# Row stores three quads later in the transfer queue, the next batches' inputs loaded a block earlier, and a run of GpSimd subtractions moved forward

## Chip, core and metric

The kernel runs on one core of a Trainium2 chip. The metric is the device time of one execution in microseconds (us), taken as the median of several runs. A profiled execution is one run of its own, with its own time.

The core's engines are TensorE (PE in the rows, PEld for its weight loads), VectorE (DVE), ScalarE (ACT), GpSimd (POOL) and SyncE (SP), which here only issues transfers and waits. Each engine has one instruction queue and works through it in order; engines meet at semaphores.

## What is computed

Four batches of 512 tokens of width 128 go through four pairs of a cross attention (to 32 context tokens) and a feed-forward part. The last feed-forward part is a mixture of 64 experts, six per token:

```
    x = x + jnp.tanh(g_xattn[0]) * _L0_xattn_ref(_layernorm(x, axis=-1), ctx_1024, mask_BxS2_bk0, ...)
    x = x + jnp.tanh(g_ffn[0]) * _L0_ffn_ref(_layernorm(x, axis=-1), ...)
    x = x + jnp.tanh(g_xattn[1]) * _L1_xattn_ref(_layernorm(x, axis=-1), ctx_1024, mask_BxSxS2_if1, ...)
    ...
    x = x + jnp.tanh(g_ffn[3]) * _L3_ffn_ref(_layernorm(x, axis=-1), ...)

            h = jax.nn.silu(jnp.einsum('th,eih->eti', x, eg_w)) * jnp.einsum('th,eih->eti', x, eu_w)
            routed = jnp.einsum('eti,ehi,te->th', h, ed_w, comb)
```

## The kernel before

The program is a sequence of blocks. In a block (`block_of`) a main part and side parts are woven together on each engine by hand-written step numbers: a part says `yield n`, and a side's piece due at step n is put into the queue when the main part reaches that step. At a block's end all engines meet. SP's program of a block is written out by itself: `first_loads`, then the clearing of one set of semaphores, then `sync`.

**Blocks 1 and 2, the front.** `fronts_beside_setup` runs `front` (the first cross attention, the first feed-forward part with its rounding to four bits, `fp4_quantise`, and the second cross attention) for batches 0 and 1, with `setup`, which prepares weights. `fronts_beside_route` runs `front` for batches 2 and 3, with `route_1`. The two fronts of a block are interleaved; in the rows of block 1, `work`, `region_a`, `weights` and `pt` belong to batch 1 (called A below), and `turned`, `small_f` and `rows` to batch 0 (B). `load_inputs` loads five arrays for a batch: context, turned context, two masks, and x. `front` begins by waiting for all five. `setup` on POOL scales small weights and then subtracts a row of the first expert matrix `w1` from its other rows, one 128x512 subtraction for each of eight experts (L649).

**The expert pages of the last layer.** Tokens have been scattered to HBM in the order of their experts (`sorted_3`). `pages_3` works on 28 quads of four pages of 128 rows. For quad q, PE turns the rows (`turn_rows`, L2899), multiplies each page with its expert's two matrices (`up`, L2911), two quads later turns the hidden rows (`turn_hidden`, L2922), and three quads later (DOWN_LAG) multiplies them down (`down`, L2935). ACT copies the turned rows (L2957), applies silu (L2963) and copies the turned hidden rows (L2970). DVE multiplies (L2987, L2995) and copies the result of a quad to SBUF (`copy_sum`, L3002). SP loads the rows of a quad (L2855) and stores its results to `made_3` (L2889). Rows and results have three buffers each. PE's order for a step q is page 0 to 3 of up(q), turn_hidden(q-2), down(q-3), with turn_rows(q+1) put between page 2 and page 3. SP's queue is

```
                for q in range(QUADS_3):
                    if q >= 3:
                        sp.wait_ge(s.xt, q - 2)
                        load_pages_3(sp, s, q)
                    n = q - DOWN_LAG - 1
                    if n >= 0:
                        store_rows(sp, n)
```

where `s.xt` counts turned quads, and `store_rows` waits for `copy_sum(n)`. Beside the pages runs `back` for the last batch (the third feed-forward part's experts and the fourth cross attention), with its steps three pages apart (`paced`).

Of the kernel before, what the change touches and what calls it, by code (L numbers as in the profile page):

```python
# [17 lines left out]
I32 = mybir.dt.int32  # L18
# [7 lines left out]
K = 32  # L26
NK2 = S + K
E8 = 8
# [19 lines left out]
QUADS_3 = (K6 * GT3 + E3) // 4  # L48
# [20 lines left out]
def flamingo_kernel(nc, a, at, early_at, out):  # L69
    with ExitStack() as ctx:  # L70
# [27 lines left out]
        def bank(i, n=1):  # L98
            return psum[:, 512 * i:512 * (i + n)]
# [12 lines left out]
        def part(region, offset, shape):  # L112

            n = int(np.prod(shape[1:]))
            v = region[0:shape[0], offset:offset + n]
            if len(shape) == 3:
                v = v.rearrange("p (a b) -> p a b", a=shape[1])
            if len(shape) == 4:
                v = v.rearrange("p (a b c) -> p a b c", a=shape[1], b=shape[2])
            return v  # L120
# [122 lines left out]
        def front_tail_of(acc):  # L243
# [9 lines left out]
                       mask1=part(turned, 1536, [P, T, K]).bitcast(I32))  # L253
# [21 lines left out]
        def back_norm(region, offset):  # L275
# [21 lines left out]
        lg = sb("lg", [P, T, E3])  # L297
        lge = sb("lge", [P, T, E3])
        gmask = sb("gmask", [P, T, 8])
        comb = sb("comb", [P, T, E3])  # L300
# [11 lines left out]
                       big_f=part(wide_2, 0, [P, T, 512]), kblk1=part(wide_2, 2048, [P, H1, K]), vo1=part(wide_2, 2560, [P, 4, D]),  # L312
                       qt_f=xnt, pt_f=part(ysb_flat, 0, [P, 2, 512]), y1_f=y1s[0], vblk1=part(wide_2, 3072, [P, H1, K]),
                       mask1=part(ysb_flat, 0, [P, T, K]).bitcast(I32))
        w_at = front_tail + FRONT_SMALL
        front_w2 = record(stats=part(region_a, w_at, [P, T, 6]), mv=part(region_a, w_at + 24, [P, T, 2]),
                          rstd=part(region_a, w_at + 32, [P, T]), rtmp=part(region_a, w_at + 36, [P, T]),
# [162 lines left out]
        def load_first_matrices(sp, s):  # L480

            for e in range(E8):
                sp.dma_start(w1[:, e, 0:F1], a["w1"][:, e, :]).then_inc(s.w1_in, 16)
                sp.dma_start(last_row(e), a["w1"][D - 1:D, e, :].broadcast_to([D, F1])).then_inc(s.w1_in, 16)

        def clear_sorted(sp, s):

            sp.wait_ge(s.cleared, 1)
            for rows in sorted_1:
                sp.dma_start(rows.rearrange("(n p r) d -> p n (r d)", p=P, r=4),  # L490
                             over(kctx[:, :, :].rearrange("p c k -> p (c k)"), 1, [P, PAGES // 4, 4 * D])).then_inc(s.rows_out, 16)

        def setup(s):
# [135 lines left out]
            def gpsimd(pool):  # L629
                yield 0  # L630
                nc.gpsimd.memset(neg_half[:, :], -0.5)
                nc.gpsimd.memset(mean_col[:, :], 1.0 / F1).then_inc(s.zeroed, 1)
                pool.wait_ge(s.front_in, all_front)
                nc.gpsimd.tensor_scalar(bq1s[:, :], bq1[:, :], float(HD1) ** -0.5, None, ALU.mult)
                nc.gpsimd.tensor_scalar(wq0s[:, :], bq0[:, :], float(D) ** -0.5, None, ALU.mult).then_inc(s.small, 1)
                yield 11
                pool.wait_ge(s.moe1_in, 16)
                nc.gpsimd.tensor_scalar(g1s[:, :], g1[:, :], float(F1) ** 0.5, None, ALU.mult).then_inc(s.g1_scaled, 1)
                pool.wait_ge(s.rest_in, all_rest)
                nc.gpsimd.tensor_scalar(rtmp[:, 0:1], wl1[:, :], 0.125, None, ALU.mult).then_inc(s.wl1_scaled, 1)  # L640
                nc.gpsimd.tensor_scalar(wgate2[:, :], wgate2[:, :], wl2[:, 0:1], None, ALU.mult)
                nc.gpsimd.tensor_scalar(wg2[:, :, :], wg2[:, :, :], wl2[:, 0:1], None, ALU.mult)
                nc.gpsimd.tensor_scalar(wu2[:, :, :], wu2[:, :, :], wl2[:, 0:1], None, ALU.mult)
                nc.gpsimd.tensor_scalar(sgu2[:, :, :], sgu2[:, :, :], wl2[:, 0:1], None, ALU.mult)
                for e in range(E8):
                    yield 20 + e
                    if e == 0:
                        pool.wait_ge(s.w1_in, 16 * 2 * E8)
                    nc.gpsimd.tensor_tensor(w1[:, e, 0:F1], w1[:, e, 0:F1], last_row(e), ALU.subtract)  # L649

            return record(tensor=tensor, vector=vector, scalar=scalar, gpsimd=gpsimd)
# [2206 lines left out]
        def pages_3(s, s_late):  # L2858

            gate_up = region_a[:, 0:2 * CH3 * 512].rearrange("p (a n) -> p a n", a=2)  # L2860
            TURN_LAG, DOWN_LAG = 2, 3
# [13 lines left out]
            def sync(sp):  # L2875
                for q in range(QUADS_3):
                    if q >= 3:
                        sp.wait_ge(s.xt, q - 2)
                        load_pages_3(sp, s, q)
                    n = q - DOWN_LAG - 1  # L2880
                    if n >= 0:
                        store_rows(sp, n)
                for n in range(QUADS_3 - DOWN_LAG - 1, QUADS_3):
                    store_rows(sp, n)

            def store_rows(sp, n):
# [190 lines left out]
        def fronts_beside_setup():  # L3077
            k = next_block()
            s0 = sems(k % 2, SETUP)
            sf = sems(k % 2, FRONT, s0)  # L3080
            sg = sems(k % 2, FRONT, sf)

            def sync(sp):
                load_front_weights(sp, s0)
                load_inputs(sp, sf, 0, front_1)
                load_inputs(sp, sg, 1, front_2)
                load_other_weights(sp, s0)
                load_first_matrices(sp, s0)
                clear_sorted(sp, s0)
                sp.wait_ge(s0.rows_out, 32)  # L3090
            block_of(k, sync, front(sf, 0, bank(0), front_1, set_f), [setup(s0), front(sg, 1, bank(3), front_2, front_w2)])

        def fronts_beside_route():
            k = next_block()
            sf = sems(k % 2, FRONT)
            sg = sems(k % 2, FRONT, sf)
            sr = sems(k % 2, ROUTE_1, sg)
            sw = sems(k % 2, ("table_in",), sr)
            s_pages = sems(1 - k % 2, PAGES_1)

            def first_loads(sp):
                load_inputs(sp, sf, 2, front_1)
                load_inputs(sp, sg, 3, front_2)

            def sync(sp):
                sp.wait_ge(sf.inputs, 5 * 16)
                sp.wait_ge(sg.inputs, 5 * 16)
                lo = early_at["b1"][0]
                sp.dma_start(w1[D - 1:D, :, 0:F1],
                             a["early"][0:E8, lo:lo + F1].rearrange("(o e) f -> o e f", o=1)).then_inc(sw.table_in, 16)  # L3110
                lo = at["be2"][0]
                sp.dma_start(be2_rows[:, :, :], over(a["weights"][0:E8, lo:lo + D], 0, [P, E8, D])).then_inc(sw.table_in, 16)
                sp.wait_ge(sw.table_in, 32)
                sp.wait_ge(scattered_1[0], 16 * K1 * GT)
                for q in range(3):
                    load_pages(sp, s_pages, q)
            block_of(k, sync, front(sf, 2, bank(0), front_1, set_f),
                     [front(sg, 3, bank(1), front_2, front_w2), route_1(sr, 0, bank(2), lambda n: 2 * n, 4)], first_loads)

        def moe_1_pages():  # L3120
            k = next_block()
# [103 lines left out]
        for b in range(B):  # L3225
            k = next_block()
# [121 lines left out]
```

## Time and profile before

| | |
|---|---|
| median of 3 runs | 1887.72 us (1884.27 to 1894.0) |
| profiled execution, its own time | 1881.52 us |
| its span, first to last instruction | 1879.7 us |
| mean granted TensorE clock | 0.929 |
| PE busy | 1614.8 us (86%) |
| DVE, POOL, ACT busy | 62%, 45%, 41% |
| block 1 | about 0.7 to 111.2 us |
| block of the expert pages | about 1569 to 1785.6 us |

A busy share says how long an engine had an instruction in work, not what the end waited for. The granted clock is 1.0 at 2.4 GHz and 0.5 at 1.2 GHz.

### The profile page before, as it was taken

The page shows a single profiled execution, that of the slowest core. Times are in us where ns is not written, and L with a number is a line of the kernel's source. Part 1 is how long each engine was busy: PE and PEld are TensorE (multiplying, and loading weights), DVE is VectorE, ACT ScalarE, POOL GpSimd, SP SyncE. Part 2 cuts the span into 40 slices and gives each one's busy share as a digit, 9 for nine tenths or more (in the row PEclk, how much of TensorE's full clock was granted, in tenths as well). Part 3 has the DMA queues.
Part 4 walks back from the last instruction along what each step waited for, and adds up shares of the span by engine and source line. Part 5 has one row for each costly group of instructions (what it writes and reads, how often), then busy time and mean ns, then how long its engine had stood idle before and what let it go on. Part 6 is the DMA issues. An engine that isn't in the chain of part 4 may idle for free. (4 is left out here: it accounts for less than half of the span.)

```text
span 1879.7 us, 30972 instructions
## 1 busy us (share of the span) xinstructions
PE 1614.8 (86%) x10175; PEld 1106.4 (59%) x10175; DVE 1171.0 (62%) x3120; ACT 772.6 (41%) x1974; POOL 848.6 (45%) x1075
## 2 busy tenths in 40 slices
PE   6755699899999999998999978699899996776699
PEld 4544477557756577564775645456577565555556
DVE  6957569767566577564784754677477473332357
ACT  2321244356446465373661742222366274222222
POOL 3441744357565386571874730127266471000072
PEclk8866799999999999999999979799999998877899
DMA  9010122100000500000000010144000004222253
GB/s 332 17 28 1 39 88 77 35 6 7 1 1 2 164 8 1 1 1 2 11 1 1 2 46 1 51 150 134 12 1 1 18 2 157 68 59 65 80 156 116
DMA packets 79564, 91.34 MB, mean 49 GB/s; under 512 B 10872, under 2 KB 57592, under 8 KB 78480
## 3 DMA queue, kind: packets, MB, share of 16 engines
q1 hardware_dynamic: 74288, 78.86, 13.6%
q0 software_dynamic: 5120, 10.50, 1.9%
q8 instruction: 86, 1.41, 0.3%
q14 instruction: 70, 0.57, 0.1%
HBM read 69.14 MB, written 27.66 MB: 51 GB/s over the span
## 5 line engine op out<-in xcount | busy, mean ns | idle before, releaser
L1672 POOL TENSOR_TENSOR rows<-rows,rinv 128x512 f32<-128x512 f32 x192 | 198.7, 1063 | 117.2 <-DVE rinv L1912 117.2
L1836 ACT ACTIVATE rows<-psum,nmax 128x512 f32<-128x512 f32 x192 | 130.0, 683 | 122.1 <-DVE nmax L1905 122.0
L2021 POOL TENSOR_TENSOR rows<-rows,rinv 128x128 f32<-128x128 f32 (+2 forms) x192 | 127.4, 685 | 77.9 <-DVE rinv L2190 77.9
L1904 DVE TENSOR_REDUCE lg<-psum 128x2 f32<-128x1024 f32 x128 | 155.7, 1216 | 3.2
L2185 DVE TENSOR_REDUCE nmax<-psum 128x1 f32<-128x128 f32 (+3 forms) x256 | 113.6, 485 | 42.7 <-PE psum L2067 41.7
L1916 DVE COPY turned<-psum 128x512 f32<-128x512 f32 x128 | 88.2, 689 | 80.3 <-PE psum L1732 79.3
L1720 PE MATMUL psum<-region_a,region_b 64*128 64x256 f32 x1024 | 130.6, 391 | 6.0 <-ACT rows L1836 2.9
L1753 PE MATMUL psum<-turned,region_a 128*64 128x256 f32 x1024 | 124.6, 385 | 0.4
L2064 PE MATMUL psum<-region_a,region_b 64*128 64x128 f32 (+2 forms) x896 | 107.2, 353 | 9.8 <-ACT rows L2137 3.7
L1720 PEld LDWEIGHTS psum<-region_a,region_b 64*128 64x128 f32 x1024 | 92.8, 186 | 28.9 <-ACT rows L1836 7.7
L1732 PEld LDWEIGHTS psum<-weights,rows 128*128 128x128 f32 x768 | 82.0, 140 | 44.9 <-issue 20.7
L1732 PE MATMUL psum<-weights,rows 128*128 128x128 f32 x768 | 103.3, 279 | 3.8 <-ACT turned L1845 2.4
L2137 ACT ACTIVATE rows<-psum,nmax 128x128 f32<-128x128 f32 (+2 forms) x192 | 96.1, 509 | 12.1 <-DVE nmax L2185 12.1
L1753 PEld LDWEIGHTS psum<-turned,region_a 128*64 128x64 f32 x1024 | 68.6, 136 | 47.1 <-issue 19.6
L2579 ACT ACTIVATE region_b<-psum 128x512 f32<-128x512 f32 x66 | 39.4, 598 | 138.0 <-PE psum L2541 138.0
L1845 ACT ACTIVATE turned<-psum 128x512 f32<-128x512 f32 x128 | 76.7, 599 | 46.0 <-PE psum L1732 46.0
L2064 PEld LDWEIGHTS psum<-region_a,region_b 64*128 64x128 f32 x896 | 70.2, 189 | 34.1 <-issue 11.8
L2553 PEld LDWEIGHTS psum<-region_c,region_b 128*128 128x128 f32 x512 | 66.0, 192 | 28.0 <-issue 22.7
L2079 PE MATMUL psum<-weights,rows 128*128 128x128 f32 x448 | 76.6, 281 | 6.8 <-DVE region_a L2196 1.7
L2987 DVE TENSOR_TENSOR region_b<-region_b,psum 128x256 f32<-128x256 f32 x28 | 11.8, 421 | 110.3 <-ACT region_b L2963 110.2
L1698 PE MATMUL psum<-kvt,weights 128*128 128x512 f32 x128 | 65.8, 643 | 11.3 <-PEq L760 7.7
L2957 ACT ACTIVATE weights<-psum 128x512 f32<-128x512 f32 x28 | 16.7, 597 | 135.4 <-PE psum L2899 135.4
(853 smaller groups left out, 4040.5 us busy)
## 6 DMA issues: line engine op xcount, KB each, us to landing
pt<-gates SPq DMA_DIRECT2D x64, 128.0 KB
ysb<-gates SPq DMA_DIRECT2D x64, 128.0 KB
weights<-sorted SPq DMA_DIRECT2D x28, 256.0 KB, 3.2
made<-weights SPq DMA_DIRECT2D x28, 256.0 KB, 2.4
sorted<-sorted SPq DMA_DIRECT2D x4, 1536.0 KB, 13.5
region_a<-in_eg SPq DMA_DIRECT2D x16, 256.0 KB, 4.3
region_a<-in_eu SPq DMA_DIRECT2D x16, 256.0 KB, 3.6
region_c<-in_weights SPq DMA_DIRECT2D x16, 256.0 KB, 5.7
```

The lines of the kernel that those rows point to most:

```text
L1672: nc.gpsimd.tensor_tensor(row(u, j), row(u, j), rinv[:, 2 * u + j:2 * u + j + 1].broadcast_to([P, S]), ALU.mult).then_inc(s.pn, 1)
L1720: mm = nc.tensor.matmul(s_bank(u, j)[:, 256 * half:256 * (half + 1)], qtt[lo:lo + 64, p, P * t:P * (t + 1)], ktt[lo:lo + 64, p, 256 * half ...
L1732: mm = nc.tensor.transpose(turn_bank(place(n, i))[:, P * k:P * (k + 1)], row(u, j)[:, P * k:P * (k + 1)], ident[:, :])
L1753: nc.tensor.matmul(bank(7)[lo:lo + HD2, 256 * half:256 * (half + 1)], vtok[:, k, P * p + lo:P * p + lo + HD2], turned2[:, 2 * half + j, k, :],
L1836: nc.scalar.activation(row(u, j), s_bank(u, j), ACT.Exp, bias=nmax[:, 2 * u + j:2 * u + j + 1], accum_out=sum_column(u // T, u % T, j)).th ...
L1845: nc.scalar.activation(turned_to(n, i), turn_bank(place(n, i)).rearrange("p (k q) -> p k q", q=P), ACT.Copy).then_inc(s.ca, 1)
L1904: link(nc.vector.tensor_reduce(maxima(u // T)[:, both(u), 0], both_scores(u), AX.X, ALU.max, negate=True))
L1916: nc.vector.tensor_copy(turned_to(n, i), turn_bank(place(n, i)).rearrange("p (k q) -> p k q", q=P)).then_inc(s.cb, 1)
L2021: nc.gpsimd.tensor_tensor(head, head, rinv[:, 2 * u + j:2 * u + j + 1].broadcast_to([P, keys(u)]), ALU.mult).then_inc(s.pn, 1)
L2064: nc.tensor.matmul(s_bank(u, j)[:, cols], qtt[lo:lo + 64, p, P * t:P * (t + 1)], krot[lo:lo + 64, cols], start=(h == 0), stop=True, skip_g ...
L2137: nc.scalar.activation(rows_of(u)[:, j, 0:keys(u)], s_bank(u, j)[:, 0:keys(u)], ACT.Exp, bias=nmax[:, 2 * u + j:2 * u + j + 1], accum_out= ...
L2185: nc.vector.tensor_reduce(nmax[:, 2 * u + j:2 * u + j + 1], s_bank(u, j)[:, 0:keys(u)], AX.X, ALU.max, negate=True).then_inc(s.mx, 1)
```

## The change

There are three edits.

First, in `pages_3` SP puts the store of quad n behind the load of quad n + 7, where it stood behind the load of quad n + 4. The waits are the same ones.

Second, block 1 loads the inputs of batches 2 and 3 behind its own loads. They go to arrays that block 1 does not use (`lg`, `lge`, `comb`); the x of batch 3 lies on weights that `setup` reads, so SP first waits for the two products that read them (`kv_products`). The clearing of `sorted_1` stands behind that wait now. `first_loads` of block 2 is gone, and its fronts read the new places.

Third, the eight subtractions on `w1` stood at steps 20 to 27 of block 1 and stand at step 12.

```
+        def next_inputs(n):
+            return dict(ctx_tok=lg[0:K, 2 * n:2 * n + 2, :].rearrange("p t e -> p (t e)"), ctx_t=lge[:, n, 0:K],
+                        mask0=lge[:, n, K:2 * K].bitcast(I32),
+                        mask1=comb[:, 2 * n:2 * n + 2, :].rearrange("p t (h k) -> p (t h) k", h=2).bitcast(I32))
+
+        front_3, front_4 = dict(front_1, **next_inputs(0)), dict(front_2, **next_inputs(1))
...
+                yield 12
+                pool.wait_ge(s.w1_in, 16 * 2 * E8)
                 for e in range(E8):
-                    yield 20 + e
-                    if e == 0:
-                        pool.wait_ge(s.w1_in, 16 * 2 * E8)
                     nc.gpsimd.tensor_tensor(w1[:, e, 0:F1], w1[:, e, 0:F1], last_row(e), ALU.subtract)
...
-                    n = q - DOWN_LAG - 1
+                    n = q - DOWN_LAG - 4
                     if n >= 0:
                         store_rows(sp, n)
-                for n in range(QUADS_3 - DOWN_LAG - 1, QUADS_3):
+                for n in range(QUADS_3 - DOWN_LAG - 4, QUADS_3):
                     store_rows(sp, n)
...
+                sf_next = sems(1 - k % 2, FRONT)
+                load_inputs(sp, sf_next, 2, front_3)
+                sp.wait_ge(s0.kv_products, 2)
+                load_inputs(sp, sems(1 - k % 2, FRONT, sf_next), 3, front_4)
                 clear_sorted(sp, s0)
                 sp.wait_ge(s0.rows_out, 32)
...
-            def first_loads(sp):
-                load_inputs(sp, sf, 2, front_1)
-                load_inputs(sp, sg, 3, front_2)
...
-            block_of(k, sync, front(sf, 2, bank(0), front_1, set_f),
-                     [front(sg, 3, bank(1), front_2, front_w2), route_1(sr, 0, bank(2), lambda n: 2 * n, 4)], first_loads)
+            block_of(k, sync, front(sf, 2, bank(0), front_3, set_f),
+                     [front(sg, 3, bank(1), front_4, front_w2), route_1(sr, 0, bank(2), lambda n: 2 * n, 4)])
```

The new code stands five or more lines lower in the file, so the same instruction has a higher line number after. On SP, at the start of the page block, the queue before is this (`weights<-sorted_3` is a load of a quad's rows, `made_3<-weights` a store; even_5 counts turned quads, even_14 copied results):

```order
L2473 DMA region_c<-in_weights 128x512 x8
L84 ISA x65
L2855 DMA weights<-sorted_3 128x4x128 [waits even_5] x2
L2889 DMA made_3<-weights 128x4x128 [waits even_14]
L2855 DMA weights<-sorted_3 128x4x128 [waits even_5]
```

and with the change it is this:

```order
L2478 DMA region_c<-in_weights 128x512 x8
L84 ISA x65
L2860 DMA weights<-sorted_3 128x4x128 [waits even_5] x5
L2894 DMA made_3<-weights 128x4x128 [waits even_14]
L2860 DMA weights<-sorted_3 128x4x128 [waits even_5]
```

Five loads stand ahead of the first store where two stood; from there on loads and stores alternate in both, and at the end eight stores follow one another where five did.

On POOL, in block 1, the queue from the scaled weights to the softmax of the second attention (L1088 subtracts a maximum, L1093 multiplies with a reciprocal) is before:

```order
L643 TENSOR_SCALAR weights<-weights 128x512
L644 TENSOR_SCALAR weights<-weights 128x128
L669 TENSOR_SCALAR region_a<-region_a 128x4
L670 TENSOR_TENSOR region_a<-region_a,neg_half 128x4
L669 TENSOR_SCALAR rtmp_f<-mv_f 128x4
L670 TENSOR_TENSOR rstd_f<-rtmp_f,neg_half 128x4
L649 TENSOR_TENSOR region_a<-region_a,region_c 128x512 x4
L1088 TENSOR_TENSOR weights<-weights,region_a 128x512
L1088 TENSOR_TENSOR rows<-rows,small_f 128x512
L649 TENSOR_TENSOR region_a<-region_a,region_c 128x512
```

and with the change:

```order
L649 TENSOR_SCALAR weights<-weights 128x512
L650 TENSOR_SCALAR weights<-weights 128x128
L654 TENSOR_TENSOR region_a<-region_a,region_c 128x512 x6
L654 TENSOR_TENSOR region_a<-region_a,region_b 128x512 x2
L674 TENSOR_SCALAR region_a<-region_a 128x4
L675 TENSOR_TENSOR region_a<-region_a,neg_half 128x4
L674 TENSOR_SCALAR rtmp_f<-mv_f 128x4
L675 TENSOR_TENSOR rstd_f<-rtmp_f,neg_half 128x4
L1093 TENSOR_TENSOR weights<-weights,region_a 128x512
L1093 TENSOR_TENSOR rows<-rows,small_f 128x512
```

All eight subtractions stand ahead of the two reciprocal deviations (L669 and L670 before); four of them stood behind those, and four stood singly in the softmax.

On SP, at the end of block 1, the queue before ends with the clearing, and block 2 begins with ten loads:

```order
L484 DMA region_b<-in_w 128x512
L490 DMA sorted_0<-kctx 128x6x512
L490 DMA sorted_1<-kctx 128x6x512
L760 UNCONDITIONAL_BRANCH
L761 UNCONDITIONAL_BRANCH
L456 DMA turned<-in_ctx 32x128
L456 DMA small_f<-in_ctx_t 128x32
L456 DMA small_f<-in_mask_keys 128x32
L456 DMA turned<-in_mask_BxSxS_if 128x4x32
L456 DMA x<-in_x 128x4x128
```

With the change, the last rows of block 1 and the first of block 2 are:

```order
L462 DMA lge<-in_ctx_t 128x32
L462 DMA lge<-in_mask_keys 128x32
L462 DMA comb<-in_mask_BxSxS_if 128x4x32
L462 DMA weights<-in_x 128x4x128
L496 DMA sorted_0<-kctx 128x6x512
L496 DMA sorted_1<-kctx 128x6x512
L765 UNCONDITIONAL_BRANCH
L766 UNCONDITIONAL_BRANCH
L84 ISA x65
L3114 DMA region_a<-in_early 1x8x512
```

The ten loads stand ahead of the clearing now, and block 2 begins with the clearing of its semaphores.

## Rows read from the trace of the kernel before

**Rows 1.** PE's waits, 1597 to 1773.1: line, releaser, us, times, longest.

```profile
PE psum L2899 <- DMA weights<-sorted: 47.4, 22, 3.8
PE psum L2935 <- ACT region_b L2970: 8.3, 12, 3.6
PE psum L2911 <- ACT weights L2957: 2.5, 9, 0.3
```

**Rows 2.** Windows: length, busy PE, PEld, DVE, ACT, POOL (instructions), clock, DMA share, GB/s.

```profile
1579.72:1587.41 7.69, 6.36 (x52) 5.54 (x50) 4.89 (x17) 3.12 (x7) 0.00 (x0) 1.00 0.17 47
1597.80:1773.02 175.22, 118.86 (x627) 97.54 (x627) 55.70 (x114) 38.57 (x77) 2.47 (x4) 0.80 0.24 67
```

**Rows 3.** Timeline, SP, DVE and PE, one quad: start, duration, engine, instruction, idle before.

```profile
1754.74 0.36 SPq L2889 DMA_DIRECT2D made<-weights  x1
1755.14 0.51 SPq L2855 DMA_DIRECT2D weights<-sorted  x1
...
1758.38 0.66 PE L2899 MATMUL psum<-weights 128*128 128x128 f32 x4 [2.23 <-DMA weights<-sorted]
...
1766.03 0.44 PE L2899 MATMUL psum<-weights 128*128 128x128 f32 x2 [3.76 <-DMA weights<-sorted]
```

**Rows 4.** Transfers by line: count, KB each, median us from issue to landing.

```profile
weights<-sorted SPq DMA_DIRECT2D x28, 256.0 KB, 3.2
made<-weights SPq DMA_DIRECT2D x28, 256.0 KB, 2.4
```

**Rows 5.** PE groups, 1597.80 to 1773.02: busy us, mean ns, idle before.

```profile
L2922 PE MATMUL psum<-weights,region_b 128*128 128x128 f32 x88 | 29.3, 333 | 0.0
```

**Rows 6.** Timeline, PE, pages at the lower and the full clock.

```profile
1616.64 0.63 PE L2911 MATMUL psum<-region_a,weights 128*128 x2
...
1617.71 0.64 PE L2911 MATMUL psum<-region_a,weights 128*128 x2
...
1760.99 0.39 PE L2911 MATMUL psum<-region_a,weights 128*128 x2
...
1761.55 0.39 PE L2911 MATMUL psum<-region_a,weights 128*128 x2
```

**Rows 7.** Timeline, seam of blocks 1 and 2: DVE, SP, PE.

```profile
110.71 0.48 DVE L1053 SCALAR_TENSOR_TENSOR x<-turned,gate,x 128x256 f32<-128x256 f32 x1
119.25 0.28 DVE L956 BATCH_NORM_STATS2 region_a<-pt 32x6 f32<-32x128 f32 x1 [8.05 <-DMA weights<-in_x]
...
111.47 0.34 SPq L456 DMA_DIRECT2D turned<-in_ctx  x1
```

**Rows 8.** Timeline, POOL, block 1.

```profile
49.97 0.76 POOL L644 TENSOR_SCALAR weights<-weights 128x128 f32<-128x128 f32 x1
65.42 0.23 POOL L669 TENSOR_SCALAR region_a<-region_a 128x4 f32<-128x4 f32 x1 [14.69 <-DVE region_a L662]
...
69.29 4.94 POOL L649 TENSOR_TENSOR region_a<-region_a,region_c 128x512 f32<-128x512 f32 x4
...
92.57 1.27 POOL L649 TENSOR_TENSOR region_a<-region_a,region_b 128x512 f32<-128x512 f32 x1
```

**Rows 9.** Timeline, DVE, block 1: the same operations alone and beside POOL.

```profile
51.02 0.17 DVE L415 TENSOR_SCALAR small_f<-small_f 128x16 f32<-128x16 f32 x1
...
54.51 0.43 DVE L425 TENSOR_SCALAR turned<-turned 128x512 f32<-128x512 f32 x1
...
67.80 1.08 DVE L680 TENSOR_SCALAR work<-x,region_a 128x128 f32<-128x128 f32 x4
69.36 4.95 DVE L680 TENSOR_SCALAR turned<-x,mv_f,rstd_f 128x128 f32<-128x128 f32 x4 [0.48 <-POOL rstd_f L670]
```

**Rows 10.** Timeline, PE, block 1.

```profile
71.20 0.60 PE L877 MATMUL psum<-weights,work 128*128 128x128 f32 x4
74.46 1.09 PE L877 MATMUL psum<-weights,turned 128*128 128x128 f32 x4 [2.66 <-DVE turned L680]
```

**Rows 11.** SP's waits, 0 to 160: line, releaser, us, times, longest.

```profile
SPq L760 <- PEq L760: 60.5, 1, 60.5
```

## The prediction

> **What bounds the kernel now.** PE is the busiest engine, so I first read what PE waits for, stage by stage, and then who releases it. In the block of the expert pages PE waits 22 times, 47.4 us in all, in front of L2899 (the turning of the next quad's rows) for the transfer that brings those rows; its two other waits there, for ACT, come to 10.8 us [rows 1]. No other stage has a wait for data that returns so often. Second comes the clock: over the same 175 us the granted clock is 0.80, where in the quads before the first store it is 1.00 [rows 2]. Third, between block 1 and block 2, DVE stands 8.05 us until the last input of batch 3 has landed [rows 7]. All three lie on the chain that sets the end: the block of the pages ends with PE, and every block starts when the last engine has left the one before.
>
> **Why the loads are late.** The SP queue says it. A store and the next load go out one behind the other, 1754.74 and 1755.14, and PE gets its rows at 1758.38, 3.24 us after the load's issue [rows 3]; the median landing time of a load is 3.2 us [rows 4]. That load was free to go long before: its buffer is empty once the quad three before has been turned. What held it was the store in front of it, which waits for a result made at the very step in which the next quad is turned. So each quad pays the landing time less the work of two or three pages.
>
> **The stores moved back.** Load of quad m now stands behind the store of quad m-8, whose result is copied at the start of step m-4, and waits for the turning of quad m-3, in the middle of step m-4. It goes out in the middle of step m-4 and is needed in the middle of step m-1, three quads later. A plain quad takes 7.65 - 3.76 = 3.89 us without its wait (1758.38 to 1766.03, [rows 3]), so the load has more than 11 us for 3.2 us of landing. The wait goes wholly: -47.4 us. The stores themselves are issued when they were, at the result's copy; a result buffer is needed again three quads, again 11 us or more, after its store goes out, and a store lands in 2.4 us [rows 4]. The last eight stores wait for their own results as the last five did, so the end of the block gets no tail. No instruction is added.
>
> **What the clock gives.** L2922 takes 0.27 us at the full clock and 0.42 us at the lower (2.4 and 1.2 GHz). Its mean over 88 is 333 ns [rows 5], so (333 - 270) / 150 = 42% of the pages ran at the lower one. Two successive pages start 1.07 us apart there (1616.64, 1617.71) and 0.56 us apart at full clock (1760.99, 1761.55) [rows 6]. 88 x 0.42 x 0.51 = 19 us for the pages; turning and `back` add about 10 by my count of their slower rows. The falls of the clock stand behind waits of 2 us and more. With PE busy 83% of the time (6.36 of 7.69 us) the clock was 1.00 [rows 2]. Without the waits PE would be busy 86% or more, so I expect most of this 29 us to come back. But not as time: a page at full clock meets waits for ACT of about 0.5 us a quad that the slower page hides. I build the stage from both sides. Upper end of the stage: no clock regained, 175.2 less the 45.6 us of waits inside it (47.4 less the first, 1.81) = 129.6 us. Lower end: 22 quads x 3.89 = 86 us, plus `back` on PE at full clock, 19 us by the starts of its rows, plus 3 us for the longest wait behind ACT (3.6 in [rows 1]) that stays = 108 us. Faster quads also pull the steps of `back` together, three pages being 1.7 us at least; each of its links (PE, then ACT or DVE for 0.6 to 0.7 us, then PE) fits, its softmax does not quite. I add 5 us for that, and 3 us for a clock that still falls at such places: 116 us. The term is 116 - 175.2 - 1.8 = **-61 us**, bounds -47 and -69.
>
> By the Trainium skill ("TensorE: Matmul & The Clock Gate", section "What's actually happening") the lower clock is the default and activity releases it, which speaks for the -61. A reader who distrusts it has -47 from the waits alone.
>
> **The inputs loaded ahead.** SP gave its first load at 111.47 and DVE started at 119.25 [rows 7]. With all arrays in place DVE and PE can start about half a microsecond behind SP's first row, at 112.0: -7.2 us. Block 2 is a chain from there to its scatter, so it shifts as a whole. The cover: the first load set goes behind the `w1` loads; the second and the clearing wait for a product that PE ends near 54 us; SP stood 60.5 us at the block's end waiting for PE [rows 11], so starting the clearing 20 us later costs nothing. Bounds -8 and 0 (if the last set came late after all).
>
> **The subtractions moved.** POOL is idle 14.69 us behind L644, from 50.7 on [rows 8], and the eight subtractions of 1.24 us each (4.94 for four) fill 50.7 to 60.7. POOL is not late for its next piece at 65.4. The price is on DVE. Four 128x128 operations of one source take 1.08 us alone and 4.95 us beside four subtractions: one per subtraction [rows 9]. In 51.0 to 54.9 DVE has exactly eight such operations (L415 to L425) on the chain to PE's L865. Held one by one they end with the eighth subtraction, at 60.7 and not 54.94: +5.7 us. Behind them PE is late: L865, L870, then L535's 64 products, and L877 of A, which started right behind them at 71.20, comes at 76.9. The hold of the four operations at 69.36 is gone, so L877 of B follows at once, at 77.8 where it stood at 74.46 [rows 10]: +3.4 us. In the softmax POOL is nearly full, and the subtraction at 92.57 [rows 8] stands in front of the product that PE waits for at 98: -1.3. Sum +2.1; bounds -4 (no hold, both savings kept) and +6.
>
> The Trainium skill ("GPSIMD Engine Reference", section 1, Specifications) says that POOL shares its SBUF interfaces with DVE instructions in a two-port mode or with two SBUF inputs. By it L421 is held as well: ninth in the row, some 0.4 us more, +2.5 for +2.1. It speaks against this edit, as the rows do.
>
> **Sum.** -61 - 7.2 + 2.1 = -66 us. Made against the profiled execution: 1881.5 - 66 = 1815.5. The median of the runs is 6.2 us above it: **1822 us**.
>
> **The rivals.**
> 1. The clock does not come back (chance 0.20). For: it has waits behind ACT to fall at, 10.8 us of them. Against: 1.00 in the quads without stores. Gain 47 + 5 - some 5 us of new waits in `back`: 1841 us.
> 2. `back` becomes the bound of the pages (0.09). Its links are serial over PE, ACT and DVE, and PE's wait for rows has hidden them. If the block only falls by 35 us: 1888 - 35 - 5 = 1848 us. Against: DVE is busy 55.7 and ACT 38.6 of 175 us.
> 3. DVE's hold reaches further (0.10): also the twelve small scalings behind L1017 and the next norm are late, or the inputs of batch 3 come late. The front then is +6 for -5: 1833 us.
> 4. More than forecast (0.08): the clock stays full and `back` fits everywhere; -69 - 8: 1810 us.
> 5. The other side, slower (0.02): result buffers. A store that went out later than its result would hold `copy_sum` three quads on, and with it PE's L2935. It decides only if the store is delayed past 9 us (three quads of 3.89 less 2.4); each quad then pays up to a whole landing, between 2.4 and 3.2 us [rows 4]. At 3.2 that is 24 x 3.2 = 77 us for the 47 gained, and with the front 1888 + 77 - 47 - 5 = 1913 us. Against: SP's wait ahead of each store is over before the store's own.
> 6. Nothing happens in the page block (0.02): the load's wait on turned quads is the true holder. 1883 us, as the front alone. Against: the order of SP's rows at each of 22 quads.
> The forecast has the remaining 0.49.
>
> **How the numbers follow.** The forecast's own range is 1814 to 1832. Rivals 1, 3 and 4 are neighbours, so 1808 to 1844 holds 8 in 10. A measurement of this kernel can tell about 0.5%, 9 us, from no change. Faster by more than that hold all but rivals 5 and 6: 0.96; within 0.5%: 0.02; slower: 0.02.
>
> **What would show it.** PE's wait for `weights<-sorted` falls from 47.4 us to under 3. The clock of the page block rises from 0.80 to 0.93 or more. The distance from the fifth quad's turning to the last is near 116 us; 130 means rival 1, 140 rival 2. In the SP rows a load is issued some 11 us before its L2899. DVE's first row of block 2 follows the last of block 1 within 1 us. DVE's eight small operations after 51 us stretch to 60 or 61; were they as short as before, the front would gain 10 us. The prediction is wrong if the page block's new waits on ACT or DVE pass 15 us.

## The result

| | before | changed |
|---|---|---|
| median of 4 runs | 1887.58 us (1884.27 to 1894.0) | 1814.12 us (1801.71 to 1816.75) |
| profiled execution, span | 1879.7 us | 1814.8 us |
| mean granted TensorE clock | 0.929 | 0.938 |

The ratio is 0.9594, with a 95% interval of 0.9542 to 0.9646: 73.5 us faster by the medians. The forecast was 1822 us in a range of 1808 to 1844. The total is near, but the page block gave more than was forecast and other parts less; what follows takes them apart.

The head of the changed kernel's profile page (busy time and share of each engine):

```profile
PE 1594.1 (88%) x10175; PEld 1088.8 (60%) x10175; DVE 1175.5 (65%) x3120; ACT 772.7 (43%) x1974; POOL 850.9 (47%) x1075
```

The number of PE instructions is the same as before (10175), and PE is 21 us less busy: no work went away, PE did the same matmuls at a higher clock. Most of the gain is in the page block. The waits of PE in it, first turning to last (line, releaser, us, times, longest); then the window from the sixth quad's turning to the last, with its clock in the third column from the right; then the groups that answer to [rows 4, 5]:

```profile
PE psum L2940 <- ACT region_b L2975: 13.5, 23, 3.6
PE psum L2916 <- ACT weights L2962: 4.8, 15, 0.6
PE psum L2916 <- DMA region_a<-in_eu: 4.4, 1, 4.4
PE psum L2904 <- PEq L2002: 2.3, 1, 2.3
```

```profile
1602.74:1708.04 105.30, 91.05 (x628) 75.69 (x628) 54.63 (x113) 38.33 (x77) 2.47 (x4) 0.96 0.36 106
```

```profile
L2927 PE MATMUL psum<-weights,region_b 128*128 128x128 f32 x92 | 25.8, 280 | 0.0
```

The waits for `weights<-sorted`, 47.4 us at L2899 in [rows 1], are gone: L2904 waits once, for the block to begin. The window of 22 quads is 105.3 us where [rows 2] has 175.22: PE stands idle 14.25 us in it instead of 56.36, and is busy 91.05 instead of 118.86. So of the 70 us gained 42 us are idle time of PE and 28 us are its higher clock. The matmul of L2927 takes 280 ns on average, 333 in [rows 5].

Three plain quads in the timeline of the changed kernel, SP and PE (start, duration, engine, instruction):

```profile
1657.33 0.60 PE L2904 MATMUL psum<-weights 128*128 128x128 f32 x4
1657.96 0.36 SPq L2860 DMA_DIRECT2D weights<-sorted  x1
1660.72 0.36 SPq L2894 DMA_DIRECT2D made<-weights  x1
1661.00 0.60 PE L2904 MATMUL psum<-weights 128*128 128x128 f32 x4
1661.63 0.36 SPq L2860 DMA_DIRECT2D weights<-sorted  x1
...
1664.67 0.60 PE L2904 MATMUL psum<-weights 128*128 128x128 f32 x4
...
1668.35 0.60 PE L2904 MATMUL psum<-weights 128*128 128x128 f32 x4
```

A load now follows the turning that empties its buffer (1657.33, 1657.96), and its store follows alone, 2.8 us later. The load of 1657.96 is turned at 1668.35, 10.4 us on, where [rows 3] has 3.24. A plain quad takes 3.67 us.

The front gained less. DVE, POOL and PE of the changed kernel in block 1, and DVE at the seam:

```profile
51.99 0.69 DVE L420 TENSOR_REDUCE small_f<-turned 128x16 f32<-128x512 f32 x1
52.71 0.97 DVE L421 TENSOR_SCALAR small_f<-small_f 128x16 f32<-128x16 f32 x1
...
56.17 0.25 DVE L425 RECIPROCAL small_f<-small_f 128x16 f32<-128x16 f32 x1
56.46 1.42 DVE L427 TENSOR_TENSOR turned<-turned,small_f 128x512 f32<-128x512 f32 x1
57.91 1.37 DVE L428 TENSOR_SCALAR turned<-turned 128x512 f32<-128x512 f32 x1
...
63.52 0.43 DVE L431 TENSOR_SCALAR turned<-turned 128x512 f32<-128x512 f32 x1
...
115.22 0.48 DVE L1058 SCALAR_TENSOR_TENSOR x<-turned,gate,x 128x256 f32<-128x256 f32 x1
116.01 0.28 DVE L961 BATCH_NORM_STATS2 region_a<-lg 32x6 f32<-32x128 f32 x1 [0.31 <-PEq L765]
```

```profile
52.39 8.01 POOL L654 TENSOR_TENSOR region_a<-region_a,region_c 128x512 f32<-128x512 f32 x6
60.36 2.84 POOL L654 TENSOR_TENSOR region_a<-region_a,region_b 128x512 f32<-128x512 f32 x2
```

```profile
79.92 0.60 PE L882 MATMUL psum<-weights,work 128*128 128x128 f32 x4
80.36 0.60 PE L882 MATMUL psum<-weights,turned 128*128 128x128 f32 x4
```

Between DVE's last row of block 1 and its first of block 2 lie 0.8 us where [rows 7] has 8.5. But block 1 ends at 115.2 and not at 110.7. The run of operations behind the reduction took 3.95 us before; it takes 11.3 us here, 52.68 to 63.95. Of its ten operations eight are held, each about as long as the subtraction beside it; the reciprocal (0.25 us) and the last one (0.43 us, behind the last subtraction) are not. The eight subtractions take 10.8 us, 1.35 us each for the 1.24 of [rows 8].

The same events in both profiled executions, before and changed: DVE's first row of block 2 119.25 and 116.01 (-3.2); the first load of `sorted_1`'s rows in block 3 224.21 and 222.01 (-2.2); SP's first copy of `sorted_1` to `sorted_3` 611.01 and 612.38 (+1.4); SP's first load of `in_eg` 1104.27 and 1104.49 (+0.2); the second load of `in_weights` to `region_c` 1208.99 and 1217.31 (+8.3); the page block's first turning 1569.02 and 1577.26 (+8.2); its last turning 1773.02 and 1708.04 (-65.0); POOL's first gather behind it 1788.06 and 1722.09 (-66.0); the span -64.9. So the page block with its end gave 74.2 us, and the 8 us at 1104 to 1209 are a loss in a place that the change does not touch. One window in it (length, busy PE ..., clock), of the changed kernel and of the one before:

```profile
1120.00:1150.00 30.00, 26.62 (x79) 13.20 (x78) 10.28 (x33) 10.84 (x19) 0.00 (x0) 0.71 0.00 1
```

```profile
1120.00:1150.00 30.00, 26.88 (x113) 13.89 (x112) 14.13 (x39) 12.22 (x20) 0.00 (x0) 0.97 0.00 1
```

PE is busy for the same 26.6 to 26.9 us, with 79 instructions in one and 113 in the other: the granted clock was 0.71 here and 0.97 there. Over the whole stretch (1104.49 to 1217.31 here, 1104.27 to 1208.99 there) both have 334 matmuls, and PE is busy 85.4 us here and 78.2 us there, at a clock of 0.77 and 0.83: 7.3 of the 8.1 us. It is not a property of the change: the same changed kernel on another chip (`c1_after` below) took 104.4 us for this stretch, at a clock of 0.83.

### The profile page after: what moved, and what is told of

Read it like the earlier page. It is cut to its first block and busy times, and to the rows that moved or that the text cites. A ratio compares the mean times of both kernels' runs of the same rounds, so it can differ in the third digit from the quotient of the medians.

```text
span 1814.8 us, 30972 instructions
## 1 busy us (share of the span) xinstructions
PE 1594.1 (88%) x10175; PEld 1088.8 (60%) x10175; DVE 1175.5 (65%) x3120; ACT 772.7 (43%) x1974; POOL 850.9 (47%) x1075
## 5 line engine op out<-in xcount | busy, mean ns | idle before, releaser
L2850 POOL DMA_INDIRECT sorted<-turned,small_f x48 | 49.2, 1024 | 49.6 <-DVE small_f L2784 35.2
L1689 POOL TENSOR_TENSOR ysb<-ysb,nmax 128x128 f32<-128x128 f32 x64 | 25.9, 405 | 94.8 <-DVE nmax L1910 93.9
## 6 DMA issues: line engine op xcount, KB each, us to landing
sorted<-sorted SPq DMA_DIRECT2D x4, 1536.0 KB, 13.7
```

## The experiments

Twelve runs were made in three groups (a "call" in the expectations), each group on a chip of its own, with the kernel before beside them. The kernel before had medians of 1992.6, 1893.0 and 1988.2 us there. So totals are compared inside a group, and stages between groups. The changed kernel itself ran only in the third group. "The stage" is the one from the sixth quad's turning to the last, 175.22 us before and 105.30 us changed.

### The stores alone

```diff
-                    n = q - DOWN_LAG - 1
+                    n = q - DOWN_LAG - 4
```

> The kernel before with the stores three quads later and nothing else. Theory A (the stores carry the whole gain): the stage from the sixth quad's turning to the last falls from 175.2 to 105 us as with the full change, PE's wait for weights<-sorted is gone, and the time is 1888 less 74 = 1814 us; DVE's first row of block 2 stays at 119. Theory B (the page block gave the 61 us that the prediction put on it and the rest came from elsewhere): 1827 us. Theory C (the clock of that stage was luck of the one profiled run): the stage at 0.80 again and 130 us long, 1841 us.

1915.15 us for 1992.64, 77.5 us less; ratio 0.9618, interval 0.9589 to 0.9648. The stage (same columns as above):

```profile
1649.45:1754.40 104.95, 90.65 (x627) 75.62 (x627) 54.63 (x113) 38.33 (x77) 2.46 (x4) 0.96 0.36 105
```

This is theory A. The stores alone carry the gain in the page block, on another chip, with the stage's clock at 0.96 again; what the other two edits add to the total is not told apart from nothing by the intervals (0.9618 here, 0.9592 for the full change in the third group). B (a ratio of 0.968) lies outside the interval, and C is out: the regained clock was no luck of one run.

### The inputs alone, and the subtractions alone

> The kernel before with the inputs of batches 2 and 3 loaded in block 1 and nothing else. Theory A: the ten loads cost block 1 nothing, its last DVE row stays at 110.7 and the first of block 2 comes at 111.5 to 112.0, 7.2 us earlier than before. Theory B: the loads are what made block 1 late by 1.7 us at 42 us (they are issued from 32.8 us on, beside the loads of the first matrices): the first row of block 2 comes at 113.2 to 113.7. In the page block nothing changes (stage 175 us).

> The kernel before with the eight subtractions at step 12 and nothing else. Theory A (the subtractions hold DVE one operation each, and their own length with it, 1.36 us, is what counts): DVE's held operations after 51 us end at 62.2 us where they ended at 54.94 before (+7.3), block 1 ends 2.8 us later, at 113.5, and DVE's first row of block 2 comes at about 122. Theory B (the 1.7 us by which block 1 was late at 42 us belong to the subtractions too): the held operations end at 63.9 and the block at 115.2. Theory C (the prediction's sum, +2.1): 112.8.

The inputs alone: 1983.99 us (one run). DVE's last row of block 1 starts at 112.71 and the first of block 2 at 113.50, 0.8 us apart; the kernel with the stores alone, on the same chip and with the old inputs, has 110.21 and 118.67, 8.5 us. The gap shrinks by 7.7 us. The block itself ended late, at theory B's number. The first 1.4 us of it are not shown to be the loads': the reduction at the head of B's quantising starts at 50.30 in the profile of before, 50.92 with the stores alone, 51.69 here and 51.75 with the subtractions alone, and that kernel loads nothing ahead. Behind B's L883 the block takes 36.9 us here and 35.1 us with the stores alone, with PE busy 28.1 and 26.5 us for the same 120 matmuls, so most of this 1.7 us is clock; why it was lower here is open. The stage of the pages is 176.94 us.

The subtractions alone: 1999.18 us (one run). The reduction starts at 51.75, and the last operation of the run ends at 63.72: 11.3 us behind the reduction's end, +7.3 again, the size in theory A. The times themselves are theory B's (63.9 and 115.2 were said; block 1's last row starts at 115.53), but the late start is not the subtractions', as the inputs alone have it too. Block 1 ends 5.3 us behind the kernel with the stores alone, and the first row of block 2 comes at 124.28 for 118.67. The stage of the pages is 180.65 us: with the old order of stores it was 175.2 to 180.7 us in three profiles, with the stores one or three quads later and no wait put back 104.6 to 105.3 us in all eight.

### The subtractions behind all other work of POOL

```diff
-                yield 12
+                yield 99
                 pool.wait_ge(s.w1_in, 16 * 2 * E8)
```

> The changed kernel with the eight subtractions behind all other work of POOL in block 1. POOL ended at 106 us there; without the subtractions ahead the block runs about 7 us earlier, POOL ends at 98.7 and the eight fill 98.7 to 108.6, beside DVE work that reads PSUM. Theory A (a hold costs only where DVE has chain work with SBUF sources alone): DVE's first row of block 2 comes at 108.5 to 110 where it stood at 116.0, and the time is 6 us below the changed kernel's, about 1808. Theory B (POOL's subtractions hold the last products' DVE work too, or block 1 ends with POOL): 112 or later, 4 us below or less.

1906.57 us for 1992.64; ratio 0.9591, interval 0.9563 to 0.9618. The first row of block 2 stands at 108.89, which is theory A for the seam; its total (6 us below the changed kernel's) can't be read here, as that kernel did not run in this group. Block 1 now ends with POOL: the subtractions end 1.1 us behind DVE's last row. DVE in the last products, with POOL's subtractions running from 97.95 to 108.55:

```profile
104.46 0.42 DVE L1055 TENSOR_TENSOR pt<-psum,weights 128x256 f32<-128x256 f32 x1 [3.54 <-PE psum L904]
104.92 1.10 DVE L1058 SCALAR_TENSOR_TENSOR x<-pt,gate,x 128x256 f32<-128x256 f32 x1
106.25 0.42 DVE L1055 TENSOR_TENSOR turned<-psum,weights 128x256 f32<-128x256 f32 x1 [0.23 <-PE psum L904]
106.71 0.72 DVE L1058 SCALAR_TENSOR_TENSOR x<-turned,gate,x 128x256 f32<-128x256 f32 x1
```

The operation that reads PSUM and SBUF is not held (0.42 us). The one with both tensors in SBUF is: 1.10 and 0.72 us for 0.48 alone.

### One quad instead of three

```diff
-                    n = q - DOWN_LAG - 4
+                    n = q - DOWN_LAG - 2
```

> The changed kernel with the stores one quad later than before instead of three. Load of quad m then stands behind the store of quad m-6, whose result is copied at the start of step m-2, and is needed in the middle of step m-1: one and a half plain quads of 3.67 us, 5.5 us, for a landing of 3.0 us. Theory A (any lead above the landing time gives the whole gain): the stage from the sixth quad's turning to the last is 105 us as with three quads, PE's wait for weights<-sorted under 3 us, and the total equals the changed kernel's. Theory B (loads and stores that go out together land later, so three quads are needed): waits for rows of half a microsecond or more come back at most quads, the clock with them, and the stage is 115 us or longer.

1802.46 us for 1893.02; ratio 0.9539, interval 0.9492 to 0.9585. The stage is 105.09 us, and PE never waits for rows. That is theory A for the stage; the total can't be set beside the changed kernel's, which did not run on this chip (the ratio was 0.9594 in the result, with an interval that overlaps this one). But my lead of 5.5 us was wrong:

```profile
1647.93 0.36 SPq L2894 DMA_DIRECT2D made<-weights  x1
...
1648.34 0.51 SPq L2860 DMA_DIRECT2D weights<-sorted  x1
...
1651.89 0.60 PE L2904 MATMUL psum<-weights 128*128 128x128 f32 x4
```

This load is turned 3.55 us after its issue; the median landing is 3.2 us. Counted over the last 22 loads, the lead is 3.55 us at least and 4.9 in the median, where the full change has 10.4 and 13.3 (its last 20), and the kernel before 3.09 and 3.24 (its last 23). Between 3.24 and 4.9 us lie 70 us of the kernel.

### Seven quads

> The changed kernel with the stores seven quads later than before (four later than the change). The store of quad n then goes out behind the turning of quad n+8 in the middle of step n+7, while copy_sum of quad n+3 needs its buffer at the start of that step. Theory A (rival 5 of the prediction): each quad pays a landing, up to 3.2 us, and the stage is 105 + 22 x 3.2 = 175 us. Theory B (the late copy is what counts: 1.8 us to the turning, 0.4 us issue, 2.4 us landing, 4.6 us late on DVE, of which PE feels what is beyond its own buffers, 2 us a quad): about 150 us. Theory C (a late store is hidden by the second PSUM bank of sums): 105 to 110 us.

1898.27 us for 1893.02 (one run), the stage 194.16 us at a clock of 0.77. DVE waits in front of the result's copy, and PE behind it:

```profile
DVE weights L3007 <- DMA made<-weights: 116.4, 17, 8.2
PE psum L2940 <- DVE weights L3007: 44.0, 13, 3.7
```

No theory had a price high enough. The stage is 88.9 us longer, 5.2 us for each of DVE's 17 waits. PE's idle time makes up 59.1 us of that (73.3 for 14.25), 44.0 us of it the 13 waits for the copy, and its busy time 29.8 us (120.86 for 91.05), which is the lower clock. The prediction's fifth rival is real: its mechanism is this one, four quads later than the change has the store. What lies between was not tried.

### Waits put back at some quads

```diff
                         sp.wait_ge(s.xt, q - 2)
+                        if q >= 6 and q % 3 == 0:
+                            sp.wait_ge(s.yc, q - 4)
                         load_pages_3(sp, s, q)
```

The second of these kernels has `if q >= 17:` in its place. `s.yc` counts copied results, so the load waits for what it stood behind before the change.

> The changed kernel, where the load of every third quad (6, 9, ... 27, eight quads) waits for the copied result that it stood behind before the change, and the others go out early. Theory A (each wait for rows also costs lower clock behind it, for about its own quad): each late quad takes 7.0 us instead of 3.7, so the stage is 105 + 8 x 3.3 = 131 us, its clock falls to about 0.88. Theory B (the low clock of the stage before came from waits at every quad, a wait at every third doesn't bring it): 8 x 2.2 = 18 us, stage 123 us, clock 0.95.

> The changed kernel, where the loads of quads 17 to 27 wait as before the change and those of quads 5 to 16 go out early. Theory A (waits bring the low clock at once and only where they are): up to quad 16 the distances between turnings are those of the changed kernel at a clock near 0.95, from there those of the kernel before (7.0 to 10 us) at a clock near 0.80; stage 105 + 11 x 3.3 = 141 us. Theory B (the clock in the page block is set by what went before it or by the run): one clock in both halves, and the second half pays 11 x 2.2 = 24 us only: 129 us.

Every third quad: 1827.24 us (one run), the stage 131.20 us, clock 0.92. PE's wait for rows:

```profile
PE psum L2906 <- DMA weights<-sorted: 17.9, 8, 4.0
```

Eight waits, 17.9 us together, cost 25.9 us; PE is busy 97.86 us and not 91.05, so 6.8 us of it is clock. That is theory A's time to 0.2 us; the clock fell less than it said (0.88) and more than theory B did (0.95).

The last eleven quads: 1843.90 us (one run), the stage 134.44 us, between the theories (141 and 129). Its two halves:

```profile
1600.64:1655.20 54.56, 49.14 (x331) 39.04 (x331) 26.14 (x47) 18.27 (x38) 0.00 (x0) 0.98 0.32 92
1655.20:1735.08 79.88, 49.69 (x299) 42.54 (x297) 29.36 (x67) 20.18 (x39) 2.46 (x4) 0.85 0.25 73
```

The first half is that of the changed kernel (54.59 us, clock 0.98). In the second the waits are back, 22.5 us in 11, and with the same 299 instructions PE is busy 49.69 us where the changed kernel has 41.88 us, at a clock of 0.85 instead of 0.93. So the clock fell where the waits are and nowhere else; theory B's one clock in both halves is out. But the half costs 29.2 us more and not the 36 of theory A: a wait costs 2.7 us here, 3.2 us at every third quad, and 3.2 us (69.9 by 22) in the kernel before.

### The placement of the subtractions on one chip

> The changed kernel once more, so that the kernels of this call can be compared with it on the same chip. DVE's first row of block 2 within 1.5 us of 116.0 (the first 40 us of block 1 differed by up to 1.7 us between executions), the stage from the sixth quad's turning to the last 105 us.

> The changed kernel with the eight subtractions where they stood before the change (four behind the second norm, four singly in the softmax). Theory A (moving them cost the front some 3 us): DVE's first row of block 2 at 112.0 to 113.5 where the changed kernel has it at 116.0, and the total 3 us below the changed kernel's, less than this measurement tells. Theory B (in the whole the move is free, the later start was the spread of the block's first 40 us): 115 or later.

> The changed kernel with the eight subtractions behind all other work of POOL in block 1 and the stores one quad later than before instead of three. Theory A (both parts add): DVE's first row of block 2 at 108.9, stage 105 us, total 7 us below the changed kernel's, ratio to the kernel before 0.956 or less. Theory B (the front's gain is given back in block 2 behind other waits): first row at 108.9, but the end of block 2 no more than 3 us earlier than in the changed kernel.

> The changed kernel without the eight subtractions on the first expert matrix (they are left out). It bounds what any place for them can give. Theory A (behind all other work they cost only the 1.1 us by which POOL ends the block after DVE): DVE's first row of block 2 at 107.4 to 107.9, DVE's eight operations after the reduction as short as before (done 4.0 us after its end). Theory B (their place at the end also lengthens the last DVE rows, by 0.4 + 0.6 + 0.2 us): 106.5 or earlier.

| kernel | reduction starts | B's L882 | last row of block 1 | first row of block 2 | median |
|---|---|---|---|---|---|
| changed | 51.62 | 80.60 | 115.78 | 116.58 | 1908.11 |
| subtractions where they stood | 51.21 | 75.33 | 110.16 | 110.96 | 1908.55 |
| behind POOL's work, stores one quad later | 51.67 | 73.38 | 108.59 | 109.93 | 1905.64 |
| none (subtractions left out, one run) | 51.19 | 72.25 | 106.58 | 107.37 | 1905.42 |

The median of the kernel before was 1988.20 us; the ratios are 0.9592 (0.9567 to 0.9617), 0.9583 (0.9559 to 0.9608) and 0.9574 (0.9550 to 0.9598). At the seam the move costs 5.6 us, more than the 2.5 to 4 us expected. Without the subtractions DVE's run of operations takes 3.95 us again, so it is they that hold it, and the first row of block 2 comes as theory A said. Behind POOL's work they cost 2.6 us (109.93 for 107.37, of which 0.5 us is the later start) and not 1.1: the first row comes 1.0 us later than expected and 6.7 us before the changed kernel's. In the totals nothing of it can be told apart: the intervals overlap. The kernel with the stores one quad later and the subtractions last has the lowest median of the three, by 2.5 us, and is not shown to be faster.

Where the 5.6 us went can be followed on SP. At the first load of block 3 the kernel with the old places is still 4.3 us ahead (216.49 for 220.78); at the first store of results 0.7 us (257.41 for 258.08). The windows between these two events, of the changed kernel and of the one with the old places:

```profile
220.78:258.08 37.30, 34.87 (x240) 27.82 (x240) 26.50 (x123) 16.84 (x32) 8.57 (x11) 1.00 0.30 101
```

```profile
216.49:257.41 40.92, 37.20 (x245) 29.55 (x245) 27.45 (x125) 17.49 (x33) 8.59 (x11) 0.96 0.27 93
```

Nearly the same work took 3.6 us more, at a clock of 0.96 and not 1.00. Over all fourteen profiles this stretch took 37.3 to 37.8 us in six and 39.3 to 40.9 us in eight. The changed kernel has both: 37.3 us here and 40.9 us in the profile of the result. Why it falls to one or the other I can't say, and the clock is not all of it, as 39.3 us came twice at a clock of 1.00. The kernel with the subtractions behind POOL's work and the stores one quad later is 5.0 us ahead of the changed kernel at the first load of block 3 and 3.0 us at the first store, so block 2 does not give its gain back (theory B), but the 7 us of theory A do not reach the total.

## Why the prediction was right, and where it was off

**The stores.** The mechanism was right in each of its signs: the load is issued 10.4 us ahead or more (11 was said), the wait is gone, the block gets no tail. The step that was off is a size, the term of -61 us. The stage was put at 116 us and measured 105.3, below the lower bound of 108; with 3.3 us before it and 1.0 us behind it, of which the prediction had 1.8, the block gave 74.2 us. Two addends of the 116 failed. The plain quad was taken as 3.89 us from one quad of [rows 3], and that was one that begins behind a wait; it is 3.67 us (1657.33 to 1661.00), which makes 4.8 us over 22 quads. And of the 30 us that I put on `back`, its longest wait, its softmax and further falls of the clock, 105.3 - 22 x 3.67 = 24.6 us were there. PE's waits behind ACT in the stage rose only from 10.8 to 13.7 us, so `back` fits between the faster quads (rival 2 is out). Seen from the upper end the same miss is one of overlap: the sum took 129.6 us as the stage without its waits and let the clock give back only 13.6 us of its 29, with new waits for ACT of half a microsecond a quad (11 us in all) as a reason. Those waits came to 2.9 us, and 24.3 us came back.

**The clock.** The estimate of 29 us that the lower clock cost was close: PE's busy time in the stage fell by 27.8 us. The kernels with waits put back show the direction, from waits to clock. Rival 1, that it would not come back, is out. By the Trainium skill ("TensorE: Matmul & The Clock Gate", section "What's actually happening") activity releases the clock; the two halves of 0.98 and 0.85 in one execution agree with it.

**The inputs.** -7.2 us was said, -7.7 us is the change in the gap at the seam.

**The subtractions.** +2.1 us was said. From the reduction's start to B's L882 the kernel before takes 24.16 us (50.30 to 74.46), the changed one 28.37, and the same kernel on another chip 28.98: +4.2 to +4.9 where I had +3.4. The step that was off is the hold, +5.7 us, which was +7.3. Two things make the difference. The eight subtractions took 10.8 us and not 9.9 (+0.9): I took POOL's own times, but POOL is held too. And the run has ten operations, of which one was still to come behind the last subtraction (+0.7).

By the Trainium skill ("SBUF — State Buffer", section "Who interferes with whom"), when DVE is in a two-port mode whoever issues first has the shared pair of ports for the whole instruction and the other is blocked. For DVE the trace agrees: 1.37 us for 0.43. For POOL it agrees in part: beside DVE's 128x512 operations of 0.43 us a subtraction took 1.44 us for 1.27, beside the one of 0.69 us 1.71, and beside those of 0.17 us 1.26 to 1.27, so less than DVE's row each time.

I counted eight held operations of one source. Eight were held, but not those eight. Among mine were the reciprocal, which is not held (0.25 us), and the last, which came behind the subtractions; missing were the two with two sources in SBUF, L417 and L421, now L423 (1.19 us for 0.18) and L427 (1.42 us for 0.69): for these the rule that I weighed against my sum was right, and the row that I relied on, with operations of one source only, could not show it.

Whether the saving of 1.3 us in the softmax was there stays open: from B's L882 to the block's last row the seven profiles with the subtractions at step 12 have 34.5 to 35.2 us, and the four with subtractions in the softmax 34.8, 35.1, 36.3 (the profile of before) and 36.9. The granted clock over these four is 0.90, 0.85, 0.86 and 0.81, so the term can't be told apart from what the clock does.

**The sum.** -66 us was said for the profiled execution and -64.9 came. That is luck in part: the page block gave 13 us more, the front 2 to 3 us less, and the blocks between lost some 10 us that no term had. Nearly all of that stands in two stretches, 3.1 us in block 3 (40.9 for 37.8) and 8.1 us behind 1104, and both vary so between executions of one kernel.

## What to carry to other kernels

In a queue that holds loads and stores in order, a store that waits for a result also holds every load behind it: compare the time from a load's issue to its use with its landing time. 3.24 us for 3.2 us cost 70 us here, and 4.9 us cost nothing; more distance than that is only margin, until a result's buffer is needed again. In this stage a wait on PE cost its own length and a third to a half as much again, with the lower clock behind it (69.9 us for 45.6, 25.9 for 17.9, 29.2 for 22.5). A gain of 5 us in a short front is no more than what later blocks give or take from execution to execution (3.6 and 8 us here), so read it at the seam, and don't promise it in the total.

## What the runs showed of the hardware

Beside subtractions of 128x512 on POOL the DVE operations with their tensors in SBUF were held for about the length of a subtraction, even where DVE's has 16 columns: 0.97 to 1.20 us for 0.17 to 0.18 us. POOL pays less: 1.27 us became 1.44 beside DVE operations of 0.43 us and 1.71 beside one of 0.69 us. A reciprocal of 16 columns (0.25 us) and an operation with one tensor in PSUM (0.42 us) were not held.

In two of the three groups the kernel before took some 100 us longer than in the runs of the result. With the stores alone, SP's first load for the page block comes 55.9 us later than in the profile of before, and only 5.2 us of that are there at 1209; between the two ACT and DVE wait for a releaser that the profile calls remote, and PE for DVE. The same waits of the changed kernel in the third group, from 1264 to 1360:

```profile
ACT region_b L2584 <- remote: 55.7, 3, 28.5
DVE region_b L2630 <- remote: 46.7, 3, 32.4
```

I did not look for the cause; no conclusion above rests on that stretch.
